# Moving the stores of the first direction's turned results one chunk later in SyncE's queue

## The reference

```
x + (attention over j of x  +  attention over i of x) / 2

attention(a): q, k, v = projections of two layer norms of a (4 heads of 16)
              q, k    = q * cos + rotate_every_two(q) * sin      (the same for k)
              out     = elu(softmax(q k^T) v Wo + bo)
```

## Time and profile before

| | |
|---|---|
| median of 3 runs | 334.65 us (333.85 to 337.41) |
| the profiled execution's own time | 336.71 us |
| its span, first to last instruction | 334.6 us |
| mean granted TensorE clock over the span | 0.879 of full |
| TensorE matmul busy | 235.9 us, 70% |
| VectorE busy | 203.9 us, 61% |
| ScalarE busy | 171.3 us, 51% |
| GpSimd busy | 126.9 us, 38% |
| DMA | 15.26 MB in 34243 packets |

### The profile page before, as it was taken

One profiled execution on the slowest core, in us unless ns is written; L12 is line 12 of the kernel. 1 busy time (PEld: TensorE's weight loads), 2 busy tenths in 40 slices (PEclk: granted clock), 3 DMA queues, 4 the chain that ended last, 5 costly groups with the idle time before them and its releaser, 6 DMA issues.

```text
span 334.6 us, 7775 instructions
## 1 busy us (share of the span) xinstructions
PE 235.9 (70%) x3138; PEld 142.4 (43%) x3138; DVE 203.9 (61%) x333; ACT 171.3 (51%) x298; POOL 126.9 (38%) x104
## 2 busy tenths in 40 slices
PE   0366776886749694674259669998999867976453
PEld 0143444554425453452248335653444434445312
DVE  2668668684635453347535495899786868285333
ACT  2142554577553737183533674367447644933282
POOL 1411669114615160550040087367496971400000
PEclk9999798999996969597556989999799997997758
DMA  7510010433030303410354300000000000002002
GB/s 191 207 63 33 33 66 32 109 84 82 16 96 0 90 10 64 94 36 0 73 112 91 75 18 0 2 5 3 0 4 2 0 2 2 0 3 65 0 1 63
DMA packets 34243, 15.26 MB, mean 46 GB/s; under 512 B 31008, under 2 KB 31520, under 8 KB 34080
## 3 DMA queue, kind: packets, MB, share of 16 engines
q1 hardware_dynamic: 32480, 13.67, 16.1%
q10 hardware_dynamic: 1728, 1.10, 1.2%
HBM read 5.42 MB, written 2.10 MB: 22 GB/s over the span
## 4 chain that ended last, share of the span: by engine, by line
PE 38%; DVE 22%; ACT 17%; issue 11%; DMA 5%; SPq 5%; POOL 1%; ACTq 1%; DVEq 0%; POOLq 0%
PE ring L565 17%; PE score L565 8%; PE oz L565 4%; DMA rot_swap<-rot_sin 4%; PE ring L570 3%; PE p_turn L565 3%; SPq L537 3%; SPq L524 2%; DVE ln_v L864 2%; PE p_turn L570 2%; DVE mix L1142 2%; DVE ln_s L844 2%; ACT prob_t L1302 2%; DVE xhat L879 2%; DVE rot_sin L1006 2%
## 5 line engine op out<-in xcount | busy, mean ns | idle before, releaser
L1527 POOL TENSOR_TENSOR a_msk<-dt_fin,c_sb 128x512 f32<-128x512 f32 x32 | 39.7, 1239 | 34.4 <-DVE dt_fin L981 22.6
L1302 ACT ACTIVATE prob_t<-p_turn 128x512 f32<-128x512 f32 x32 | 17.7, 595 | 41.9 <-PE p_turn L570 41.8
L565 PE MATMUL score<-k_bd,q_rot 32*64 32x128 f32 x512 | 23.0, 330 | 17.6 <-POOL q_rot L895 16.0
L1142 DVE TENSOR_TENSOR mix<-dec,g_m 128x512 f32<-128x512 f32 x32 | 31.4, 987 | 2.2 <-ACT dec L1384 1.5
L1047 DVE TENSOR_REDUCE s_max<-score 128x16 f32<-128x1024 f32 x16 | 19.5, 1221 | 20.7 <-PE score L565 20.7
L1006 DVE SCALAR_TENSOR_TENSOR rot_cos<-ring,b_att,p_sb 128x512 f32<-128x512 f32 x15 | 11.2, 747 | 30.2 <-PE ring L565 17.2
L570 PE MATMUL ring<-c_sb,xhat 128*128 128x128 f32 x44 | 11.1, 401 | 25.1 <-DVE xhat L879 21.3
L565 PEld LDWEIGHTS score<-k_bd,q_rot 32*64 32x64 f32 x512 | 18.2, 165 | 23.5 <-POOL q_rot L895 18.2
L565 PE MATMUL score<-a_msk,c_sb 128*128 128x512 f32 x44 | 25.2, 656 | 0.0
L895 POOL TENSOR_TENSOR q_rot<-rot_cos,rot_swap 128x512 f32<-128x512 f32 x7 | 8.9, 1266 | 42.3 <-DMA rot_swap<-rot_sin 42.3
L1512 POOL TENSOR_TENSOR dtx<-xv,dt_fin 64x512 f32<-64x512 f32 x16 | 19.8, 1239 | 13.2 <-PE p_turn L565 12.2
(11 more groups left out here) (177 smaller groups left out, 582.6 us busy)
## 6 DMA issues: line engine op xcount, KB each, us to landing
rot_swap<-rot_sin SPq DMA_DIRECT2D x32, 128.0 KB, 2.1
p_sb<-params SPq DMA_DIRECT2D x1, 1520.0 KB, 9.2
x_tok<-x SPq DMA_DIRECT2D x16, 64.0 KB, 2.5
attention_j_turned<-y_tok SPq DMA_DIRECT2D x16, 64.0 KB, 2.2
back<-attention_j_turned SPq DMA_DIRECT2D x16, 64.0 KB, 2.4
ut_a<-u SPq DMA_DIRECT2D x8, 126.0 KB, 2.8
ut_b<-u SPq DMA_DIRECT2D x8, 124.0 KB, 3.1
ut_b<-u SPq DMA_DIRECT2D x8, 122.0 KB, 3.2
```

The source lines that it names most:

```text
L565: return pe.matmul(dst, lhsT, rhs, start=start, stop=stop, skip_group_check=True)
L1142: v.tensor_tensor(mix[:, e % LAPS, :, :], dec[:, e % LAPS, :, :], wide(g_m[:, e // 4 % 2, e % 4, :], SSM_H), ALU.mult)\
L1302: a.activation(prob_t[:, e % 2, 4 * hp:4 * hp + 4, :].rearrange("p k n -> p (k n)"), PT[hp], ACT.Identity)\
L1527: gp.tensor_tensor(a_msk[:, m % LAPS, :, :], deep(dt_fin[:, 0, SSM_H * m:SSM_H * (m + 1)], GRID), wide(cst("tri"), SSM_H), ALU.mult).then_ ...
```

## The change

The loop on SyncE runs over g = 0 to 4 instead of 0 to 3. The stores of result g-1 now stand in iteration g, between the key swap and the query swap of chunk 4+g; iteration 0 has no store, and iteration 4 has only the stores of result 3. No DMA is added or removed, and every wait that existed is kept with its threshold; only the place of the four groups of stores, with their waits for `y_turned`, moves.

```diff
-            for g in range(CHUNKS):
-                swap(CHUNKS + g, 0)
-                sp.wait_ge(y_turned, g + 1)
-                for a in range(2):
-                    for m in range(2):
-                        sp.dma_start(turned_w[a, m, g],
-                                     y_tok[64 * a:64 * a + 64, g, :].rearrange("p (k m c) -> p k m c", k=4, m=2)[:, :, m, :])\
-                            .then_inc(turned_out, 16)
-                swap(CHUNKS + g, 1)
+            for g in range(CHUNKS + 1):
+                if g < CHUNKS:
+                    swap(CHUNKS + g, 0)
+                if g >= 1:
+                    sp.wait_ge(y_turned, g)
+                    for a in range(2):
+                        for m in range(2):
+                            sp.dma_start(turned_w[a, m, g - 1],
+                                         y_tok[64 * a:64 * a + 64, g - 1, :].rearrange("p (k m c) -> p k m c", k=4, m=2)[:, :, m, :])\
+                                .then_inc(turned_out, 16)
+                if g < CHUNKS:
+                    swap(CHUNKS + g, 1)
```

## The result

| | before | after |
|---|---|---|
| median (runs) | 335.07 us (4) | 310.26 us (4, 308.6 to 311.72) |
| ratio, 95% interval | | 0.925 (0.9175 to 0.9326) |
| profiled execution, its span | 336.71, 334.6 us | 311.26, 309.1 us |
| mean granted clock of TensorE | 0.879 | 0.913 |

The kernel is 24.8 us faster in the medians and 25.5 us in the two spans. A second measurement of the changed kernel gave 309.90 us (six runs, 308.99 to 313.3), ratio 0.9239 (0.9194 to 0.9283).

A forecast was written before the change was run, and what follows sets the result against it. Stores waiting in SyncE's queue ahead of query swaps were taken to bound the stretch. Idle 15.98 plus clock 7.1 gave 23.1 us; 334.65 - 23.1 = 311.6, predicted as 312.0 us, range 308.5 to 319.

The forecast's parts named there:

- What bounds the kernel: Between 66 and 152 us, stores waiting for `y_turned` in SyncE's queue (40.1 us) hold query swaps, so TensorE's scores wait 16.0 us.
- Idle that goes: TensorE's idle ahead of the scores of steps 8, 10, 12 and 14 vanishes: 3.26 + 4.51 + 3.33 + 4.88 = 15.98 us.
- Clock that comes back: TensorE in steps 10, 12 and 14 returns to full clock: 2.55, 2.55 and 2.0 us, together 7.1 us.
- Steps: Scores of steps 8, 10, 12 and 14 on TensorE should stand near 81.3, 92.6, 103.9 and 115.2 us.
- Slack: Chunk 5's query sum on GpSimd ends at 87.3 or 88.8, needed at 92.6: 3.8 us to spare at the worst.
- Query swaps within 0.2 us of the end of their rotation: Sign in SyncE's queue: query swaps should start within 0.2 us of the end of the sine rotation.
- Return of the turned results: Result 3's stores near 112, first load of `back` near 116.5, first addition near 129, waiting for TensorE, not GpSimd.
- Contention: Stores right behind key swaps might slow their landing, 3.63 us instead of 2.08; slack of 3.8 us or more absorbs it.
- The clock is not given back: Rival: TensorE stays at its lower level for three even steps, only 16.0 us go, about 318.7 us; chance 0.1.
- The size: Whole-kernel gain of 23.1 us in all, idle and clock together; 312.0 us predicted.

The follow-up runs named there:

- the kernel with the wait alone: The changed kernel with each query swap again waiting for `y_turned`, the stores staying where the change put them; 312.64 us.
- the filled kernel: The kernel before, with three matmuls of constants on TensorE ahead of its wait for the query sum in steps 10, 12 and 14; 328.87 us, ratio 0.9839.

## Why the prediction was right, and where it was not

*What bounds the kernel.* Right as a place, and incomplete as a weight. The query swap in SyncE's queue was on the path, and moving the stores freed it. But I wrote that the wait for `y_turned`, 40.1 us in the queue's account, was what sat there, and did not ask what it would cost without the four stores behind it. The wait alone costs 2.1 us, four stores ahead of a ready swap nothing; one behind the other they made the 16 us, with the stores' issue about 11 of them and slower landings 2.8. A swap that waits for `y_turned` and nothing else has its sum ready 4.0 us after it (the copy ends at 90.47, the sum at 93.18 + 1.28 = 94.46 in that kernel), and TensorE itself needs 3.5 us from there to its next scores (11.3 us for the two steps, of which `y_turned` comes 7.8 into). The forecast did not depend on this split, since it was made of TensorE's idle times.

*Idle that goes, 15.98 us.* Right: no wait for the query sum is left at these four places.

*Clock that comes back, 7.1 us.* Right, 2.55 + 2.52 + 2.15 = 7.2 us: step 10 takes 6.88 us, step 12 5.82, step 14 4.84 (114.42 to 119.26). The term taken for step 14 was 2.0. The kernel with TensorE kept busy shows the same 7.2 us at these three places without the rest.

*Steps.* I put the scores at 81.3, 92.6, 103.9 and 115.2; they are at 80.59, 91.86, 103.12 and 114.42, all 0.7 to 0.8 early, of which 0.6 is an earlier step 6.

*Slack.* Right in size: four spare stores cost nothing, and twelve cost 1.6 us at the first place and more behind it. Chunk 5's sum ended at 87.15 (85.87 + 1.28) against scores at 91.86: 4.7 us. That it meets the 87.3 worked out is luck: GpSimd had its masks done at 85.00, a microsecond earlier than worked out, and then waited for the query swap, issued from 81.53 for 1.15 us, which landed late:

```profile
85.87 1.28 POOL L898 TENSOR_TENSOR q_rot<-rot_cos,rot_swap 128x512 f32<-128x512 f32 x1 [0.87 <-DMA rot_swap<-rot_sin]
```

*Query swaps within 0.2 us of the end of their rotation.* This sign held for chunks 5 and 6. Chunk 4's went out at 72.77, 2.3 us after its rotation (70.49), since the two issues of its key swap stood ahead, and chunk 7's 0.3 us after it. Neither was late for its sum.

*Return of the turned results.* Right: the last stores at 111.05 (112 forecast), loads at 115.23 (116.5), the first addition at 128.00 (129). The loads came 4.2 us after the stores and not 4.7: a landing counts from the start of an issue, and I had added it to the end.

*Contention.* I carried 2.08 and 3.63 us as landings. The row at 82.36 that I took for the query swap is the second DMA of chunk 5's key swap: it landed at 84.44, after the query sum had begun at 83.21. The query swap's own landing was the same 2.1 us, so nothing in the sum changes. And I took the 3.63 us for the work of the 16 loads behind that swap, which the runs do not bear out. The query swap at 81.53 took 3.2 us from the end of its issue (82.68) to the sum at 85.87, with nothing behind it in the queue until 88.47; in the kernel with the wait alone the last query swap (114.31 + 1.16) had four stores right behind it, and its sum began 1.5 us later, at 117.00. Late landings, up to 4.23 us and so above my upper bound, appear with and without other transfers behind, and what makes them is open. The Trainium skill, page "DMA: Bandwidth & Descriptors", section "Queues, rings and completion order", has each engine take descriptors in ring order; no run here shows a swap held back by what stands behind it, and none explains the late ones. For the scores of the changed kernel it made no difference, but it was 2.8 us of the stalls of before.

*Rivals.* "The clock is not given back" fell in this kernel: all rows at 1.10 us. But the range was right to hold it: in other kernels here the clock fell behind idle times of 2 us and less, while in the changed one no idle time in the stretch is over 1.03 us, as the reason against it had said.

*The size.* 23.1 us forecast, 23.46 in the stretch, 24.8 in the medians. The 1.4 us behind the first addition and the 0.6 ahead of step 6 were not in the sum. The instructions there are the same, and the changed kernel's own second trace has 179.1 us behind the first addition where the first had 181.1, so differences of this size are scatter and the 24.8 us are not a better number than the 23.5.

## What to carry to other kernels

A DMA queue is a program: what stands behind a wait and behind the issues of other transfers is late, however ready its data are. Put transfers whose result is needed late behind those needed now, and ask of each what it leaves ahead. A wait that is long in the queue's account can be nearly free on the path, and yet use up the room that would have hidden the issues behind it (0.65 us each here): price the two together and each alone. A stall on TensorE has a second price, the matmuls behind it at half clock, here 7 us beside 16, and it can be measured by itself by filling the stall with matmuls nobody needs. When a stall is removed, an engine that was never blamed (ScalarE here) holds the path, so moving the issues onto it gave back about half of the gain.

## What I had not expected of the hardware

The clock after a stall doesn't follow from the stall's length alone. At the first scores after idle times of 3.26 us (before, step 8) and 1.97 and 1.96 us the matmuls ran at the 2.4 GHz level; after 3.27 us (the filled kernel, step 8), 3.21 and 2.02 us at the 1.2 GHz level. After 3.55 us the scores ran fast and the matmuls behind them slow, and after 1.84 us (ScalarE's stores) the clock fell within the scores, which took 1.78 us. A price for it can only be given as "0 to 2.5 us a place" here.

Four stores in a row on SyncE mostly took 2.61 to 2.63 us to issue, but 3.22 in one group of the changed kernel and 3.53 in one with the wait alone. In long rows the median of one stays at 0.617 us, but single ones take up to 2.25 us, and the mean rises to 0.7 or 0.8 us (8.39 and 9.06 us for twelve, 12.68 for sixteen). On ScalarE four took 2.60 to 2.81 us.

The same small swap landed 2.1 us after its issue most times, and 3.3 to 4.2 us after it at some places, whatever stood behind it.
